# Gather loop of a graph-attention kernel: VectorE's four sums of a step stand in a row at its head

## The reference, cut to what matters

```python
h = features @ W_layer.T + b_layer
a1 = (h @ w_a1.T + b_a1)[:, 0]
a2 = (h @ w_a2.T + b_a2)[:, 0]
v = jax.nn.leaky_relu(a1[row] + a2[col], negative_slope=LEAKY_SLOPE)
m = jax.ops.segment_max(v, row, num_segments=n)
ev = jnp.exp(v - m[row])
s = jax.ops.segment_sum(ev, row, num_segments=n)
att = ev / s[row]
out = jax.ops.segment_sum(att[:, None] * h[col], row, num_segments=n)
```

## Time and profile before

| | before |
|---|---|
| timed runs, median (lowest to highest) | 2673.71 us (2671.26 to 2674.08) |
| the profiled execution, its own time | 2673.89 us |
| its span | 2672.2 us |
| gather stage in it (first gather at step 8 to last sum) | 409.6 to 1711.8 us |
| busy over the span: PE, DVE, ACT, POOL | 84%, 66%, 47%, 48% |
| mean granted clock of TensorE | 0.884 of full |

### The profile page before, as it was taken

One profiled execution on the slowest core, in us unless ns is written; L12 is line 12 of the kernel. 1 busy time (PEld: TensorE's weight loads), 2 busy tenths in 40 slices (PEclk: granted clock), 3 DMA queues, 4 the chain that ended last, 5 costly groups with the idle time before them and its releaser, 6 DMA issues.

```text
span 2672.2 us, 44967 instructions
## 1 busy us (share of the span) xinstructions
PE 2246.7 (84%) x12642; PEld 1845.2 (69%) x12659; DVE 1756.8 (66%) x5731; ACT 1261.8 (47%) x3795; POOL 1289.9 (48%) x1320
## 2 busy tenths in 40 slices
PE   3789848887788888888777788869999999999997
PEld 1566626665566666665555566667999999999997
DVE  8677747777777777777777776777555555555553
ACT  7666645555555555555555555651222222222221
POOL 0000045666666666666666666007444444444443
PEclk8899958788988888788999987659999999999999
DMA  2243333443444344443444435590222222222221
GB/s 80 91 137 120 123 87 93 111 108 109 114 112 111 106 112 114 112 109 110 112 114 112 108 106 86 109 326 16 35 37 33 36 35 35 37 35 35 37 35 27
DMA packets 141978, 237.84 MB, mean 89 GB/s; under 512 B 29546, under 2 KB 101066, under 8 KB 140970
## 3 DMA queue, kind: packets, MB, share of 16 engines
q0 software_dynamic: 65664, 143.64, 24.4%
q1 hardware_dynamic: 76074, 91.34, 10.4%
HBM read 182.34 MB, written 52.53 MB: 88 GB/s over the span
## 4 chain that ended last, share of the span: by engine, by line
PE 49%; DVE 23%; issue 13%; another core or an unknown queue 5%; DVEq 4%; ACT 3%; DMA 2%; POOL 0%; SPq 0%; ACTq 0%; POOLq 0%
PE psum L1695 19%; PE psum L1728 10%; DVE arena L1291 9%; PE psum L1195 7%; DVEq L1310 3%; PE psum L524 3%; PE psum L1203 2%; PE psum L1187 1%; DVE arena L1302 1%; DVE arena L1361 1%; DVE arena L1333 1%; PE psum L503 1%; DVE arena L1355 1%; DMA arena<-mix_inputs 1%
## 5 line engine op out<-in xcount | busy, mean ns | idle before, releaser
L1149 POOL DMA_INDIRECT arena<-table,arena x878 | 854.4, 973 | 483.0 <-issue 250.9
L1195 PE MATMUL psum<-arena 128*128 128x257 f32 x1756 | 652.0, 492 | 254.5 <-DVE arena L1291 156.3
L1195 PEld LDWEIGHTS psum<-arena 128*128 128x128 f32 x1756 | 338.6, 228 | 469.5 <-issue 372.9
L1291 DVE SCALAR_TENSOR_TENSOR arena<-arena,psum 128x257 f32 x878 | 420.5, 479 | 308.2 <-remote 181.1
L1695 PE MATMUL psum<-arena 128*128 128x128 f32 x4620 | 550.8, 275 | 0.6 <-ACT arena L1750 0.6
L1695 PEld LDWEIGHTS psum<-arena 128*128 128x128 f32 x4620 | 541.4, 192 | 6.7 <-issue 0.9
L1825 POOL DMA_INDIRECT out<-arena x105 | 170.6, 1625 | 382.1 <-ACT arena L1757 379.1
L1222 ACT ACTIVATE arena<-arena 128x128 f32<-128x128 bf16 x880 | 280.9, 390 | 119.3 <-DVE arena L1305 69.8
L1728 PE MATMUL psum<-arena 128*128 x1260 | 290.7, 379 | 0.8 <-ACT arena L1757 0.8
L1235 ACT ACTIVATE arena<-arena 128x128 f32<-128x128 bf16 x880 | 281.2, 391 | 7.1
L1187 PEld LDWEIGHTS psum<-arena 128*128 128x128 f32 x1760 | 244.2, 209 | 23.8 <-issue 18.0
(11 more groups left out here) (344 smaller groups left out, 3127.1 us busy)
## 6 DMA issues: line engine op xcount, KB each, us to landing
mix_inputs<-arena SPq DMA_DIRECT2D x147, 128.0 KB, 2.2
arena<-table,arena POOLq DMA_INDIRECT x878
arena<-in_x SPq DMA_DIRECT2D x98, 128.0 KB, 2.9
arena<-mix_inputs SPq DMA_DIRECT2D x49, 256.0 KB
arena<-in_w SPq DMA_DIRECT2D x6, 1364.0 KB, 6.5
out<-arena SPq DMA_DIRECT2D x50, 128.0 KB, 3.2
table<-arena SPq DMA_DIRECT2D x49, 129.0 KB, 2.2
arena<-mix_inputs SPq DMA_DIRECT2D x49, 128.0 KB, 3.2
```

Of the source, the lines that this page charges most:

```text
L1149: pool.indirect_dma_start(rows_in[j][:, q * TW:(q + 1) * TW], None, table_d[:, :], bass.IndirectOffsetOnAxis(ap=col_all[:, t:t + 1], axis=0))\
L1195: last = mm(psum[4 + q][:, 0:C + 1], weight[b][:, q * P:(q + 1) * P], rows_in[g][:, q * TW:q * TW + C + 1], start=True, stop=True)
L1291: v.scalar_tensor_tensor(here, here, alpha[(j - 5) % RING][:, q:q + 1], psum[4 + q][:, 0:C + 1], ALU.mult, ALU.add).then_inc(S("acc_done"), 1)
```

## The change

In DVE's step the four sums, which stood among the small instructions of the scores, the maximum, the scan and the shifts, now follow one another at the head of the step. Nothing is removed or added; every semaphore and every count stays.

```diff
                 if due(i):
                     dve.wait_ge(S("pe_step"), i)
-                add(i, j, 0, columns)
+                for q in range(G):
+                    add(i, j, q, columns)
                 exponents(i, j, 0)
                 if live(i, 1):
                     b, t = (j - 1) % 2, i - 1
                     v.tensor_copy(lb[b][:, 0:G], a1t[:, ds(t * G, G)])
-                add(i, j, 1, columns)
                 exponents(i, j, 1)
...
                 exponents(i, j, 2)
-                add(i, j, 2, columns)
                 if live(i, 1):
                     dve.wait_ge(S("max_done"), t + 1)
...
                     v.tensor_tensor(mix_b[m % MS], psum[3][:, C:2 * C], mix_b[m % MS], ALU.add).then_inc(S("half_ready"), 1)
-                add(i, j, 3, columns)
                 if live(i, 1):
                     dve.wait_ge(S("lin_steps"), t + 1)
```

## The result

| | before | after |
|---|---|---|
| median of four timed runs | 2673.56 us | 2693.32 us |
| lowest to highest | 2671.26 to 2674.08 us | 2692.26 to 2698.34 us |
| ratio, with its 95% interval | | 1.0078 [1.0064, 1.0091] |
| span of the profiled execution | 2672.2 us | 2690.5 us |
| end of the last sum, the end of the gather stage | 1711.77 us | 1730.11 us |

The last two lines place the loss: all 18.3 us lie before the end of the gather stage, none behind it. (2673.71 us, given for the kernel before above, is the median of three of these four runs.)

The account below looks back on a forecast made before the run. The gather stage was taken to be bound by the loop POOL, semaphore, POOL at 12.0 us per two steps. 2673.89 us plus 13 us of DVE overflow, other terms at nothing, gave 2687, rounded to 2686 for the median; range 2668 to 2745.

Parts of the forecast that it names:

- Sums in a row and the tail: DVE's step: dependent sums start 0.617 us apart, so the tail comes 0.82 us later, about 0.7 with mix.
- DVE's floor against 12.0 us a pair, with the late semaphores on top: Gather stage: DVE's pairs grow to 10.94 and 11.44 us; with delays the latter overflow by 0.24 us, 13 us in all.
- one delay of 0.8 us: DVE's tail: assumed late-semaphore delay per pair, a little over the mean of about 0.7 us.
- A sign read at the wrong steps: DVE's timeline: if right, the first sum of odd steps would wait mostly 0.4 to 0.5 us.
- The pairs of the sum (1 and 2, 3 and 0): DVE steps modulo 4 held by POOL's 12.0 us: 1 and 2 without mix, 10.94 us; 3 and 0 with it, 11.44.
- The end of the stage: Last gather steps, outside POOL's pace: 0.8 us each in three or four, 2 to 3 us, inside the rounding.
- PE: PE's products in the gather stage: much of their 156.3 us wait for the sums goes; gain costed at nothing.
- Faster through PE: Rival: POOL waits for PE's step, so its earlier end saves 0.3 us a pair, 32 us: 2641 us; chance 0.13.
- absorbed: Rival: POOL's 12.0 us a pair hold and hide DVE's added length: 2674 to 2677 us; chance 0.32.
- the outright bound: Rival: DVE becomes the bound, pairs of steps 3 and 0 taking 13.6 us, 86 us more: 2760; chance 0.14.
- ACT "just in time", at nothing: ACT's exponential argument comes 1.4 us later, its weights done at about 5.4 us, just in time for PE; costed at nothing.
- The rule on waits: Rival from the skill text: semaphores make DVE's chained sums no slower, so pairs stay as before, 2674 us; chance 0.03.

Follow-up runs that it names:

- chip A: Chip of the main result, no edit: the kernel before 2673.56 us, the change 2693.32 us.
- chip C: Chip of the second follow-up set, both kernels rerun without an edit: the kernel before 2657.29 us, the change 2673.67 us, ratio 1.0064.
- the narrow sums: The changed kernel with each sum 65 columns wide instead of 257, also called the change with narrow sums: 2659.55 us, ratio 1.001, on chip C.
- the row behind the maximum: The changed kernel with its four sums in a row moved behind scores, maximum and subtraction: 2672.98 us, ratio 1.0063, on chip C.
- the three sums at the head: The kernel before with sums 0 to 2 in a row at the head, sum 3 in its old place: 2688.77 us, ratio 1.0044.
- the sign first: The changed kernel with ACT's sign matrix made before its weights: 2598.25 us, ratio 1.0539, on chip B; 2697.83 us, ratio 1.0076, on another chip.
- chip B: Chip of the first follow-up set, where the kernel before took 2462.56 us; the change without further edits wasn't run there.
- narrow sums: The kernel before, old order, with each sum 65 columns wide instead of 257: 2458.58 us, ratio 0.9977, on chip B.
- the two edited kernels with short steps: The kernel before on chip B, with sums 65 columns wide (2458.58 us) and with sum 1 right behind sum 0 (2474.16 us).

## Why the prediction was right, and where it wasn't

- **Sums in a row and the tail.** Right: 0.613 us apart (predicted 0.617), L1353 3.74 us after the first sum (3.75), the step 5.48 us (5.47).
- **DVE's floor against 12.0 us a pair, with the late semaphores on top.** Right in kind, and near in size: 0.24 us in four steps were predicted and 2 x (12.125 - 12.007) = 0.24 measured on chip A, though chip C gives 0.12. That it is the length which costs is shown by the narrow sums (other length, same order, no steady loss), and the row behind the maximum agrees (same length, other order, same time). That the size hit so well is luck in good part. I took one delay of 0.8 us for a spread from 0 to over 2, and let the pairs with mix alone overflow. They lose 0.19 us each on chip A (groups 10 to 198), but those without mix lose 0.06, and on chip C both lose some 0.05; the three sums at the head overflow by nearly as much where that arithmetic allows nothing. And I took the 12.0 us for a rigid pace that stays; on chip A the change breaks it up into pairs of 11.1 to 13.6 us.
- **A sign read at the wrong steps.** I wrote that the first sum of odd steps would wait mostly 0.4 to 0.5 us, and that the late semaphore comes at even ones. Those are POOL's groups; DVE's steps have it the other way round. In DVE's even steps 86 of 97 waits are of that size, in the odd ones 47 of 97. The pairs of the sum (1 and 2, 3 and 0) were the right ones.
- **The end of the stage.** Here the forecast fell short. I priced "three or four" steps at 2 to 3 us, "inside the rounding". Beyond group 218 it is seven steps, not paced by POOL. DVE's rows of L1272 there, before and after:

```profile
L1272 DVE SCALAR_TENSOR_TENSOR arena<-arena x8: 154/156/158, 1671.4 to 1705.3; 128x4 f32<-128x4 f32 x8
```

```profile
L1272 DVE SCALAR_TENSOR_TENSOR arena<-arena x8: 162/163/164, 1684.3 to 1723.8; 128x4 f32<-128x4 f32 x8
```

  Seven intervals take 33.9 us before and 39.5 after: 5.6 us, 0.80 a step, the same number as in the tail of one step; most of the other 1.4 lies between the gather of group 218 and the first of these rows. On chip C it is 32.0 and 40.1, so 8.1 or 1.16 a step, which is more than the length: steps of 6.36 us beside those of 5.5 say that late semaphores strike there too. The term that was mis-sized is this one: 7.0 us in place of 2 to 3, which I then did not even add. 2673.89 + 12.2 + 7.0 - 0.9 gives the 2692.2 of the profiled execution.
- **PE.** The fall of its wait for the sums was right, and that it gains nothing too. "Faster through PE" did not come, nor did "absorbed" (2674 to 2677) or the outright bound (2760) on this chip.
- **ACT "just in time", at nothing.** Right in the sum, wrong as a picture: PE waits 207.9 us at L1187, much of it for what ACT makes of the late maximum. The row behind the maximum and the sign first show that this wait takes the place of another one, and in the change with narrow sums it stands at 127 us and costs the steady part nothing. In the kernel with three sums at the head the weights do come late for PE (112.9 us), so the cover is thin.
- **The rule on waits** that I set against the trace (the Trainium skill, VectorE: DVE Perf Modes, section The DRAIN you can't avoid) would have given no change. The row of four sums in the middle of the stage, 0.613 us from start to start against 0.40 to an instruction that waits for nothing, and the 0.8 us a step that followed from it, decide against it for this kernel.
- **What I took for a fixed thing.** The 12.0 us are not the kernel's pace but that of the kernel on some chips. On chip B DVE's floor and POOL's own 10.0 us nearly coincide, and a row of sums (with the sign first) costs 5.4%, not 0.8%. What makes the difference between the chips is open, beyond that it takes the four transfers of a group to bring it out.

No version here is faster than the kernel before on the same chip without leaving work out. Where DVE is shortened (narrow sums, 2458.58 against 2462.56 us) POOL's issue takes over within 0.2%.

## What to carry to other kernels

Small dependent instructions and long ones that wait for one another are each other's cover: putting the long ones in a row exposes the links on both sides (0.21 us for each pair of sums, and the waits of the tail), here 0.8 us in a step of 4.65. Before such a step is lengthened, compare the engine's spare time at the head of the step, less what always passes there, with what is added, and look separately at the stretch where the pacing engine has finished, because there every step pays in full. Don't count on the spare time to the last tenth: here the loss began before it was used up. And a pace that comes from late semaphores belongs to the chip: an order that costs 0.8% under it cost 5% without it (in the kernel with the sign first).

## What was not expected of the hardware

- The same program takes 2462.56 us on one chip and 2657 to 2676 us on others, the larger part of it in the gather stage (pairs of groups 10.09 to 10.19 us in the two edited kernels with short steps there, 11.86 to 12.01 in the kernel before elsewhere). With half of the gathers the chips agree: 2438.81 and 2439.62 us.
- On the slower kind semaphores of PE and DVE arrive up to some 2.5 us late, about every 12 us in the kernel before, and in these runs only with all four gathers of a group. ACT's own chain shows none: its weights wait for its exponential and start 0.03 us after it each time (7.1 us of idle time in all). In the kernel before on chip C the waits for "remote" at DVE's first sum add up to 176.5 us; in the traces of chip B there is no such row.
- The distance of two dependent sums is their duration and 0.13 to 0.15 us at both widths: 0.613 for 0.48 us (257 columns), (1.56 - 0.28) / 3 = 0.427 for 0.28 us (65 columns).
